# Searching token numbers for four expert tiles together in a mixture-of-experts kernel

## The reference

```python
topk_w, topk_idx = _route(x, w_router, b_router)   # 8 experts of 64 for each token
sort = jnp.argsort(topk_idx.reshape(-1))           # (token, expert) pairs, ordered by expert
tok = sort // TOPK
x_sorted = x_flat[tok]
g = jax.lax.ragged_dot(x_sorted, we_gate, group_sizes)
u = jax.lax.ragged_dot(x_sorted, we_up, group_sizes)
o = jax.lax.ragged_dot(jax.nn.silu(g) * u, we_down, group_sizes)
y = jnp.zeros_like(x_flat).at[tok].add(o * w_sorted[:, None])
```

## Time and profile before

| | |
|---|---|
| median of 3 runs | 4144.19 us |
| the profiled execution's own time | 4155.44 us |
| its span in the trace | 4153.6 us |
| mean granted TensorE clock | 0.966 of full speed |
| TensorE products busy | 3764.9 us (91%) |
| VectorE busy | 2483.5 us (60%) |
| ScalarE, GpSimd busy | 1349.8 us (32%), 1602.7 us (39%) |

### The profile page before, as it was taken

The page is one execution under the profiler, slowest core; times in us unless marked ns, Lnnn a source line. Parts: engine busy times, 40 slices in busy tenths (PEclk is TensorE's granted clock), DMA queues, the critical chain, the costliest instruction groups (busy, mean ns, idle before and its releaser), DMA issues.

```text
span 4153.6 us, 114223 instructions
## 1 busy us (share of the span) xinstructions
PE 3764.9 (91%) x16852; PEld 2848.1 (69%) x16853; DVE 2483.5 (60%) x6804; ACT 1349.8 (32%) x4031; POOL 1602.7 (39%) x1208
## 2 busy tenths in 40 slices
PE   6729999959999999999999899999999999999997
PEld 3305454437777777777777777777777777777785
DVE  5365555556666666666666566666665666666653
ACT  2212222213333333333333333333333333333332
POOL 1100000004444544445444444444444445444443
PEclk9859999979999999999999999999999999999998
DMA  3422323225666666666565656566556566666654
GB/s 116 105 62 89 95 94 92 87 74 113 146 132 129 144 143 120 145 133 156 115 132 117 162 117 132 115 139 137 117 117 134 116 156 143 131 131 146 129 101 76
DMA packets 216178, 502.41 MB, mean 121 GB/s; under 512 B 46587, under 2 KB 46715, under 8 KB 215360
## 3 DMA queue, kind: packets, MB, share of 16 engines
q0 software_dynamic: 129024, 320.94, 41.5%
q1 hardware_dynamic: 86592, 177.77, 12.8%
q10 hardware_dynamic: 512, 3.15, 0.4%
HBM read 1115.65 MB, written 191.41 MB: 315 GB/s over the span
## 4 chain that ended last, share of the span: by engine, by line
PE 53%; DVE 7%; issue 7%; ACT 4%; DVEq 4%; ACTq 2%; DMA 1%; POOLq 0%; POOL 0%; SPq 0%
PE e_ps_gu L1430 31%; PE e_ps_y L1447 14%; PE e_ps_x L1407 4%; DVE e_w_low L1559 4%; ACT e_w_high L1496 3%; PE e_ps_h L1457 2%; PE e_ps_find L1414 2%; DVEq L1301 1%; DMA out<-e_y,e_y_ids 1%; ACT e_xT_high L1504 1%; ACTq L1301 1%; DVE e_below L1599 1%; DVE e_y L1586 1%; DVEq L1559 0%; ACT e_silu L1515 0%
## 5 line engine op out<-in xcount | busy, mean ns | idle before, releaser
L1381 POOL DMA_INDIRECT out<-e_y,e_y_ids x576 | 937.5, 1628 | 1500.2 <-ACT e_weight L1508 806.8
L1430 PE MATMUL e_ps_gu<-e_w_high,e_xT_high 128*128 x2304 | 694.9, 423 | 32.8 <-issue 15.9
L1373 POOL DMA_INDIRECT e_x<-token_rows,e_x_ids x576 | 615.0, 1068 | 275.1 <-issue 267.7
L1430 PE MATMUL e_ps_gu<-e_w_high,e_xT_low 128*128 x2304 | 641.1, 400 | 0.0
L1430 PE MATMUL e_ps_gu<-e_w_low,e_xT_high 128*128 x2304 | 640.1, 400 | 0.0
L1586 DVE TENSOR_SCALAR e_y<-e_ps_y,e_weight 128x512 f32 (+1 forms) x576 | 430.4, 747 | 247.7 <-PE e_ps_y L1447 228.4
L1567 DVE TENSOR_TENSOR e_xT_low<-e_ps_x,e_xT_high 128x512 fp32r<-128x512 f32 x576 | 398.1, 691 | 261.0 <-ACT e_xT_high L1504 179.4
L1515 ACT ACTIVATE e_silu<-e_ps_gu 128x256 f32<-128x256 f32 x576 | 222.1, 386 | 968.5 <-PE e_ps_gu L1430 904.9
L1430 PEld LDWEIGHTS e_ps_gu<-e_w_high,e_xT_low 128*128 128x128 f32 x2304 | 439.4, 191 | 108.3
L1430 PEld LDWEIGHTS e_ps_gu<-e_w_low,e_xT_high 128*128 128x128 f32 x2304 | 438.7, 190 | 106.8
L1430 PEld LDWEIGHTS e_ps_gu<-e_w_high,e_xT_high 128*128 128x128 f32 x2304 | 392.4, 188 | 132.0 <-issue 52.5
(11 more groups left out here) (245 smaller groups left out, 4315.7 us busy)
## 6 DMA issues: line engine op xcount, KB each, us to landing
e_w_raw<-in_L_ffn_we_gate SPq DMA_DIRECT2D x576, 512.0 KB
e_w_raw<-in_L_ffn_we_up SPq DMA_DIRECT2D x576, 512.0 KB
e_w_raw<-in_L_ffn_we_down SPq DMA_DIRECT2D x576, 512.0 KB
a_x<-in_L_attn_x SPq DMA_DIRECT2D x64, 256.0 KB, 3.5
t_x_in<-in_L_attn_x SPq DMA_DIRECT2D x64, 256.0 KB, 2.8
token_rows<-t_xn SPq DMA_DIRECT2D x64, 256.0 KB, 3.1
out<-t_y_out SPq DMA_DIRECT2D x64, 256.0 KB, 2.0
e_x<-token_rows,e_x_ids POOLq DMA_INDIRECT x576
```

What stands on the lines that cost most here:

```text
L1373: pool.indirect_dma_start(x[:, s % XS, :], None, k.rows, bass.IndirectOffsetOnAxis(x_ids[:, s:s + 1], 0)) \
L1381: pool.indirect_dma_start(k.out, bass.IndirectOffsetOnAxis(y_ids[:, s:s + 1], 0), y[:, s % YS, :], None, compute_op=ALU.add).then_inc(adde ...
L1430: last = nc.tensor.matmul(ps_gu[s % 2][:], x[:, s % 2, c, :], w[:, c], start=(n == 0), stop=(n == 3 * DC - 1))
```

## The change

The comparison is made once for four tiles (a `past` of four slots, one tensor_tensor of 64 x 4 x 128), at the end of VectorE's fourth step of four. The search runs 12 tiles ahead instead of 8. TensorE reads the four experts' numbers after gate_up in the first step of four (experts_of), and makes the four products in a row in the second step, between turn_x and gate_up, into two banks of ps_find with two tiles each. VectorE takes two tiles in its second step and two in its third, with one `rest` and one final sum for each two. For the second bank of ps_find, ps_x gives up one of its two: turn_x(i+1) now waits for keep_low(i).

```diff
@@ -1201,7 +1201,7 @@
     XS, YS = 8, 8
-    AHEAD_FIND, AHEAD_IDS, AHEAD_X = 8, 7, 5
+    AHEAD_FIND, AHEAD_IDS, AHEAD_X = 12, 7, 5
     AHEAD_W, WS = 6, 4
     RETIRE = 3
     with ExitStack() as ctx:
@@ -1230,15 +1230,15 @@
         hT_high = sb("hT_high", [P, 2, FC, P], F32R)
         hT_low = sb("hT_low", [P, 2, FC, P], F32R)
         y = sb("y", [P, YS, D])
-        past = sb("past", [NB, 2, P], BF16)
-        rest = sb("rest", [P, 2])
-        below = sb("below", [P, P])
-        tokens = sb("tokens", [P, 2])
+        past = sb("past", [NB, SHORT, P], BF16)
+        rest = sb("rest", [P, SHORT])
+        below = sb("below", [P, 2, P])
+        tokens = sb("tokens", [P, SHORT])
         tile_ids = sb("tile_ids", [P, TABLE])
-        ps_x = [ps(f"ps_x{i}", [P, DC, P]) for i in range(2)]
+        ps_x = ps("ps_x", [P, DC, P])
         ps_gu = [ps(f"ps_gu{i}", [P, 2, F]) for i in range(2)]
         ps_h = ps("ps_h", [P, FC, P])
-        ps_find = ps("ps_find", [P, P + 2])
+        ps_find = [ps(f"ps_find{i}", [P, 2, P + 2]) for i in range(2)]
         ps_y = [ps(f"ps_y{i}", [P, D]) for i in range(2)]
 
         w_loaded = [sem(f"w_loaded{i}") for i in range(WS)]
@@ -1401,19 +1401,27 @@
 
             def turn_x(i, s):
                 pe.wait_ge(gathered[s % XS], 16 // XS * (i - s % XS) + 16)
-                after(pe, xT_low_ready, i - 1)
+                after(pe, xT_low_ready, i)
                 chunks = x[:, s % XS, 0:D].rearrange("p (q c) -> p c q", c=DC)
                 for c in range(DC):
-                    last = nc.tensor.transpose(ps_x[s % 2][:, c, :], chunks[:, c, :], k.ident[:])
+                    last = nc.tensor.transpose(ps_x[:, c, :], chunks[:, c, :], k.ident[:])
                 last.then_inc(xt_done, 1)
 
-            def find(i, s):
-                e = pe.snap(entry(pe, i, 0, 2 * WSLOTS * E - 1) // (2 * WSLOTS), min_val=0, max_val=E - 1)
-                pe.wait_ge(marked, i + 1)
+            def experts_of(i):
+                return [pe.snap(entry(pe, i + t, 0, 2 * WSLOTS * E - 1) // (2 * WSLOTS), min_val=0, max_val=E - 1)
+                        for t in range(SHORT)]
+
+            def find(i, experts):
+
+
+                pe.wait_ge(marked, i + SHORT)
                 after(pe, picked, i)
-                nc.tensor.matmul(ps_find[:], past[:, s % 2, :],
-                                 k.ranks[:, bass.ds(e, 1), :].rearrange("j o t -> j (o t)"), start=True,
-                                 stop=True).then_inc(found, 1)
+                for t, e in enumerate(experts):
+                    last = nc.tensor.matmul(ps_find[t // 2][:, t % 2, :], past[:, t, :],
+                                            k.ranks[:, bass.ds(e, 1), :].rearrange("j o t -> j (o t)"), start=True,
+                                            stop=True)
+                    if t % 2 == 1:
+                        last.then_inc(found, 2)
 
             def gate_up(i, s):
                 place = words.place(s)
@@ -1464,18 +1472,21 @@
                     words.load(i, s)
                 if exists(i + 1):
                     turn_x(i + 1, (s + 1) % UNROLL)
-                if exists(i + AHEAD_FIND):
-                    find(i + AHEAD_FIND, (s + AHEAD_FIND) % UNROLL)
+                if s % SHORT == 1 and exists(i - 1 + AHEAD_FIND):
+                    find(i - 1 + AHEAD_FIND, held[0])
                 gate_up(i, s)
                 if s + 1 < UNROLL:
                     words.load(i + 1, s + 1)
+                if s % SHORT == 0 and exists(i + AHEAD_FIND):
+                    held[0] = experts_of(i + AHEAD_FIND)
                 if exists(i - 1):
                     turn_h(i - 1, (s - 1) % UNROLL)
                 if exists(i - 2):
                     down(i - 2, (s - 2) % UNROLL)
 
-            for i in range(AHEAD_FIND):
-                find(i, i)
+            held = [None]
+            for i in range(0, AHEAD_FIND, SHORT):
+                find(i, experts_of(i))
             turn_x(0, 0)
             walk(pe, step)
             turn_h(TILES - 1, UNROLL - 1)
@@ -1501,7 +1512,7 @@
                 e = act.snap(words.expert(s), min_val=0, max_val=E - 1)
                 act.wait_ge(xt_done, i + 1)
                 after(act, gu_done, i - 1)
-                nc.scalar.copy(xT_high[:, s % 2], ps_x[s % 2][:]).then_inc(xT_high_ready, 1)
+                nc.scalar.copy(xT_high[:, s % 2], ps_x[:]).then_inc(xT_high_ready, 1)
                 after(act, retired, i - YS + 2)
                 nc.scalar.copy(y_ids[:, bass.ds(slot, 1)], tile_ids[:, bass.ds(i, 1)])
                 after(act, y_made, i - SHORT + 1)
@@ -1564,7 +1575,7 @@
             def keep_low(i, s):
                 v.wait_ge(xT_high_ready, i + 1)
                 after(v, gu_done, i - 1)
-                nc.vector.tensor_tensor(xT_low[:, s % 2], ps_x[s % 2][:], xT_high[:, s % 2].bitcast(F32),
+                nc.vector.tensor_tensor(xT_low[:, s % 2], ps_x[:], xT_high[:, s % 2].bitcast(F32),
                                         ALU.subtract).then_inc(xT_low_ready, 1)
 
             def keep_h_low(i, s):
@@ -1586,22 +1597,26 @@
                 nc.vector.tensor_scalar(y[:, bass.ds(slot, 1), :].rearrange("p o d -> p (o d)"), ps_y[s % 2][:],
                                         weight[:, s % SHORT:s % SHORT + 1], None, ALU.mult).then_inc(y_made, 1)
 
-            def mark(i, s):
-                after(v, found, i - 1)
-                nc.vector.tensor_scalar(past[:, s % 2, :], k.slot_row[:], k.begin[:, bass.ds(i, 1)], None,
-                                        ALU.is_ge).then_inc(marked, 1)
-
-            def pick(i, s):
-                v.wait_ge(found, i + 1)
-                nc.vector.tensor_tensor(rest[:, s % 2:s % 2 + 1], k.rank[:, bass.ds(i, 1)],
-                                        ps_find[:, P:P + 1], ALU.subtract)
-                v.drain()
-                nc.vector.scalar_tensor_tensor(out=below[:], in0=ps_find[:, 0:P],
-                                               scalar=rest[:, s % 2:s % 2 + 1], in1=k.last_weight[:], op0=ALU.is_le,
-                                               op1=ALU.mult, accum_out=tokens[:, s % 2:s % 2 + 1])
-                v.drain()
-                nc.vector.tensor_tensor(tile_ids[:, bass.ds(i, 1)], tokens[:, s % 2:s % 2 + 1],
-                                        ps_find[:, P + 1:P + 2], ALU.add).then_inc(picked, 1)
+            def mark(i):
+
+                nc.vector.tensor_tensor(past[:], k.slot_row[:].unsqueeze(1).to_broadcast([NB, SHORT, P]),
+                                        k.begin[:, bass.ds(i, SHORT)].unsqueeze(2).to_broadcast([NB, SHORT, P]),
+                                        ALU.is_ge).then_inc(marked, SHORT)
+
+            def pick(i, t):
+
+                v.wait_ge(found, i + t + 2)
+                nc.vector.tensor_tensor(rest[:, t:t + 2], k.rank[:, bass.ds(i + t, 2)], ps_find[t // 2][:, :, P],
+                                        ALU.subtract)
+                v.drain()
+                for u in range(2):
+                    nc.vector.scalar_tensor_tensor(out=below[:, u], in0=ps_find[t // 2][:, u, 0:P],
+                                                   scalar=rest[:, t + u:t + u + 1], in1=k.last_weight[:],
+                                                   op0=ALU.is_le, op1=ALU.mult,
+                                                   accum_out=tokens[:, t + u:t + u + 1])
+                v.drain()
+                nc.vector.tensor_tensor(tile_ids[:, bass.ds(i + t, 2)], tokens[:, t:t + 2], ps_find[t // 2][:, :, P + 1],
+                                        ALU.add).then_inc(picked, 2)
 
             def step(i, s, slot):
                 if s == 0:
@@ -1611,10 +1626,10 @@
                     keep_low(i + 1, (s + 1) % SHORT)
                     split_low(i + 1, (s + 1) % SHORT, 0)
                 split_low(i, s, 1)
-                if exists(i + AHEAD_FIND):
-                    pick(i + AHEAD_FIND, s)
-                if exists(i + AHEAD_FIND + 1):
-                    mark(i + AHEAD_FIND + 1, s + 1)
+                if s in (1, 2) and exists(i - s + AHEAD_FIND):
+                    pick(i - s + AHEAD_FIND, 2 * s - 2)
+                if s == SHORT - 1 and exists(i + 1 + AHEAD_FIND):
+                    mark(i + 1 + AHEAD_FIND)
                 hidden(i, s)
                 if exists(i - 1):
                     keep_h_low(i - 1, (s - 1) % SHORT)
@@ -1622,10 +1637,11 @@
                     scale(i - 2, (s - 2) % SHORT, slot(UNROLL - 2))
 
             v.sem_inc(w_low_ready[1], 1)
-            mark(0, 0)
-            for i in range(AHEAD_FIND):
-                mark(i + 1, i + 1)
-                pick(i, i)
+            for i in range(0, AHEAD_FIND, SHORT):
+                mark(i)
+                pick(i, 0)
+                pick(i, 2)
+            mark(AHEAD_FIND)
             words.load(0, 0)
             split_low(0, 0, 0)
             keep_low(0, 0)
```

## The result

| | before | after |
|---|---|---|
| median | 4143.04 us (4 runs) | 4093.64 us (4 runs, 4088.80 to 4097.86) |
| profiled execution, its own time | 4155.44 | 4088.80 |
| span | 4153.6 | 4087.0 |

The ratio is 0.9871, 95% interval 0.9859 to 0.9883: faster by 1.3%. Measured again on another occasion it was 0.9872 (0.9856 to 0.9889). The forecast was 4084 us, 60 less than before; it is 49 to 53 less.

The account below looks back on a forecast made before the run. TensorE, busy 91% of the span, was taken as the bound, expert products ahead. -117 - 125 + 182 = -60 us from 4155.44 gave 4095, or 4084 us by the median; forecast's own range 4030 to 4140, over all cases 3960 to 4180.

Parts of the forecast that it names:

- 3 and 4, VectorE, ps_x: VectorE's merged comparisons, rests and sums, and ps_x in one bank: nothing; bounds 0 and -10, 0 and +15.
- Part 1: TensorE's four search products in a row, 0.09 us apart: -117 us (-87 to -131) over 141 groups.
- Part 2: Search's wait for VectorE's comparison goes, as it is made a step and more earlier: -125 us (-40 to -150).
- the weights were ready 2.5 us ahead of the gate products: At a change of expert, the reason given for taking -125 us for the removed comparison wait.
- the loop heads before: Loop heads' share of the 159.5 us lost in the expert stage before: some 15 us.
- Part 4: turn_x(i+1) waits for keep_low(i) on the single ps_x bank; slack 1.9 to 3.1 us, cost nothing (0 to +15).
- Part 5: Four table reads in TensorE's sequencer delay turn_h: 0.57 us idle in step 4, 1.43 in step 0; +182 (+115 to +311).
- slow reads: Table reads at times slow, 0.303 median but up to 1.135 us; 0.26 us added for them in eight tiles.
- The 0.17 behind each idle time: With an empty queue the first down product comes some 0.17 us later, twice in eight tiles.
- Rival A: Burst of reads hidden because the sequencer runs further ahead: 35 us instead of 182, 3937 us by the median; chance 0.15.
- the sequencer is never seen against a full queue in a searching step: Evidence offered for rival A, about TensorE's sequencer in the kernel before; no size given.
- Rival B: Slow reads meet the burst, 4.44 us lost a pass: 311 us instead of 182, 4213 us; chance 0.20.
- Rival C: Comparison's wait only moves, to VectorE's two picks or the single ps_x bank: gain only 40, 4169 us; chance 0.15.

Follow-up runs that it names:

- one bank: The kernel before with one bank of ps_x instead of two and nothing else changed: 4144.70 us, ratio 0.9983.
- two and two at the end: Changed kernel with its four table reads split into pairs behind down in two steps, products and picks one step later: 3932.8 us, ratio 0.9476 to before.
- single searches: Kernel before with the comparison two tiles ahead of its pick, two banks of ps_find, one of ps_x, single products and reads: 4079.70 us, ratio 0.9831.
- the two runs on it: Kernel before, comparison two tiles ahead: with two ps_find banks and one ps_x bank 4079.70 us, 0.9831; with that move alone 4138.44 us, 0.9969.
- the picks behind scale: Two pairs of reads at their steps' ends, plus VectorE's picks and comparison moved behind scale: 4018.33 us, ratio 0.9680 to before.
- the doubled burst: Changed kernel with each of the burst's four table reads made twice, eight in a row: 4749.49 us, ratio 1.1437 to before.

## Why the prediction was right

The forecast was 4084 us against 4093.6 measured, and the way to it holds, with terms off by 13, 30 and 17 us. That these cancel is luck. So is a part of the close match in the ledger below: it compares the two profiled executions, of which the one before lies 12 us above its median and the one after 5 below. By the medians 49 us were gained, not 60 and more, and a term below can be off by some 10 us for that reason alone. The ledger of the stage, by the starts of line 1438 (1430):

| part | forecast | found | from |
|---|---|---|---|
| 1, four products in a row | -117 | -130 | 141 x (1.46 - 0.54) |
| 2, wait for the comparison | -125 | -95 | what is left of the sum |
| 3 and 4, VectorE, ps_x | 0 | 0 | ratio 0.9983 with one bank |
| 5, burst of reads | +182 | +165 | 3132.8 - 2967.4, changed kernel less two and two at the end |
| sum | -60 | -60.5 | |

Part 1. The products stand 0.056 apart, not 0.09: the four have a duration of 0.40 together at 2558.86, one has 0.22 to 0.23 (0.40 less 0.23, in three). That was the lower bound, the spacing of the bf16 pairs with 64 columns; 66 more columns cost nothing here.

Part 2 is the term that was mis-sized. The step that failed was "the weights were ready 2.5 us ahead of the gate products, so I take -125": the comparison's wait was indeed gone, but a step with new weights does not become a plain one. Alone, in single searches, it is worth 70 us, in the changed kernel some 95 by the ledger. The two kernels differ most at the loop head: step 7 of eight holds 24 us above a plain step in the changed kernel, against 51 with single searches. Why is open. The prediction also took too little for the loop heads before: it says some 15 us, but its own 0.55 a pass makes 38 in 70 passes, and the trace has 36. And what it read as a wait for the comparison was in the main one for the pick that stands before it, as the two runs on it show; the changed kernel takes both away, so the term didn't suffer.

Even with the reads spread, 3886.1 - 918.7 - 0.7 = 2966.7 us against 575 x 4.913 + 141 x 0.54 = 2901 leave 66 us, nearly all in steps with new weights and at loop heads behind them. What holds those is open; I only know that the order of VectorE's work there matters.

Part 4 was right with its slack, and the picks behind scale show its limit.

Part 5. The mechanism was right: the place, the steps and the begin of the reads. Step 4, forecast 0.57 idle, has 0.67 (3.56 instead of 2.89, the median of 45 steps without new weights); step 0, forecast 1.43, has 1.06 (3.95, of 54), with a mean of 1.31. By gate starts, steps 0 and 4 without new weights take 6.78 and 6.22 in the median of 56 each, and 7.23 and 6.26 in the mean, where a step with four products and no burst takes 5.45. That is 2.1 in eight tiles by the median and 2.6 by the mean; the forecast had 2.34, and 2.6 with slow reads. The 0.17 behind each idle time, for which the prediction names no row, was 0.1 in step 4 and 0.3 in step 0. Little of the 165 us can be the clock: added up over stretches of 20 us, the lower level holds some 50 us in the changed kernel and 42 in the kernel before (1000 to 4000 us), and 7 with two and two at the end (1000 to 3800). The 43 us between the first and the last cost at most half of that, some 20 us; against the kernel before it is nothing.

Rival A is out: the reads were not hidden; the sequencer began them 0.1 to 0.8 ahead of the gate start (2552.95 is the gate start of a step 4 whose first read stands at 2552.2), not further ahead than the 18 pairs allow. The trace says it for every step: counted in the order of the program at each read of line 1301 in the loops, at most 17 products had not started yet, and 17 is the median at the read behind gate_up in steps 2, 3, 4 and 6 of eight. With the one that runs these are the 18 pairs. The kernel before and four of the other kernels show the same 17, never more. So the prediction's point for rival A, that the sequencer is never seen against a full queue in a searching step, was a misreading: in the kernel before the median at the search's own read is 17 in steps 3, 4, 5 and 7. At the last read of the burst none is left, in the median of either step. The Trainium skill, TensorE: Matmul & The Clock Gate, section on the 16 sub-arrays, gives the queue as 64 entries; by that rule they would have been hidden in step 4, and the trace does not agree. Rival B's price, a slow read in each burst, did not come; the doubled burst shows what it would have been. Rival C is right by a third of the way from 125 to its 40 us, but of its two reasons one is out: the single ps_x bank costs nothing, and line 1407 doesn't wait for keep_low. Whether the picks are the other is open.

## What to carry to other kernels

An engine's sequencer is a resource of its own: register reads that were hidden one by one came out when they were made in a row, so spread them, and put them where most issued work lies ahead of the engine. Making the products of four tiles in a row paid here (0.365 us each alone, 0.54 for four together); making the reads for them in a row did not. And a list of waits can name the instruction that ended last instead of the one waited for: look at what the program's order asks for. Here the merged form gives 1.3%, and with its four reads in two pairs at the ends of two steps 5.2%.

## What the runs showed of the hardware that was not expected

Idle time of TensorE can cost more than itself. With 4 us of idle in each burst the products behind it took 1.06 us for two instead of 0.63, at a granted clock of 0.50 there and of 0.91 over the loops; by difference that was about 200 us of the 650. The shorter idle time of the changed kernel (0.90 in the step 0 shown) didn't do that: the clock stood at 1.00 over the products behind it, 2535.34 to 2538.17, and over the loops at 0.99, as in the kernel before. TensorE's sequencer never ran further ahead than 18 pairs of a weight load and a product, in the kernel before and in five others. And four bf16 products of 130 columns, each with its own weight load, went 0.056 us apart, no slower than those of 64 columns in the earlier trace rows.
